# Two tiles' q in one pass group, and the projection moved to q's bank

## The chip, the cores and the metric

One core of a Trainium2 chip. The time is that of one execution on the device, in microseconds; lower is better. Five engines work side by side with queues of their own: TensorE (PE; its weight loads are shown as PEld), VectorE (DVE), ScalarE (ACT), GpSimd (POOL), and SyncE (SP), which starts the DMA transfers. They meet only by semaphores.

## The reference

The input is 8 images of 256 channels, 56 x 56, float32. Layer 0: `x = x + conv3x3(gn(x))`, where `gn` normalizes over 32 groups of 8 channels. Layer 1: `x = x + attention(gn(x))`. The attention works in windows of 4 x 4 pixels (16 tokens), 196 windows an image:

```python
qkv    = einsum('nchw,oc->nohw', windows, qkv_w)        # 256 -> 768 channels
pooled = avg_pool5(qkv)                                 # inside the window, sum / 25
q, k, v = relu(...), relu(...), ...                     # 64 groups of 8 channels: 32 of qkv, 32 of pooled
kv  = einsum('ngld,nglm->ngdm', k, [v, 1])
out = einsum('ngld,ngdm->nglm', q, kv);  out = out[..., :-1] / (out[..., -1:] + 1e-15)
y   = proj_w @ out                                      # 512 -> 256 channels, then batch norm
```

## The kernel before, in words

The images are done one after the other. An image has two parts. The **convolution** runs in 4 chunks of 14 rows, each as 4 products (a transform of the three columns of taps saves a third of the work); a product is, for each half `mt` of the output channels, 18 TensorE passes of 392 columns. Its operands are float32 values divided into a high and a low part (`F32R`, one pass each), and high x high, high x low and low x high are added (`PARTS`). The **attention** runs over 25 tiles (`TILES`) of 8 windows, 128 tokens; the last, tile 24, has 4 windows, 64 tokens. Products of the next image's first chunks are laid beside the ends of the attention: product halves stand in tiles 0, 22, 23 and 24, and `first_chunk` mixes the first tiles' work with the next image's first products. The last image has no products left; there `keep_warm` fills the beginning.

TensorE's order in a turn of the attention (`tile`, turn s): `attend` (q of tile s times its kv; 64 small matmuls of two passes), `keys_times_values` for tile s+1, `q_of_tile` for tile s+2, `turn` (transposes what VectorE divided, `ao`), `pooled` (pooling of tile s+2's keys and values), `project` of tile s-1, `keys_values` of tile s+3. Turns 1 to 20 are a hardware loop of 10 rounds with two turns each; the others are written out. `at_slot` places the code of some turns at an offset (`SLOT_...`). A float32 matmul, as in `q_of_tile` and `project`, is two passes in the trace; one with F32R operands is one.

ScalarE in turn s: `pooled_q` of s+1 (two instructions out of `qsum`), `turned` (the copy of the transposed result to `at`), `pooled_keys_values` of s+2, `q_of_tile` of s+2 (a raw copy to `qraw`, and two masked relus from PSUM), `batch_norm` of s-1, `split_tile` of s+4 (high part of the normalized tile), `keys_values` of s+3. VectorE: `weights` and `outputs` of s (den, rcp, ao), `kv_low_part` of s+2, two `mask` of s+1, `normalize_tile` and `tile_low` of s+4. A tile whose 8 windows cross a row of 14 windows is normalized and added in 4 instructions, another in 2; tiles 1, 3, 5, 8, 10, 12, 15, 17, 19 and 22 cross one. GpSimd: `spread_pooled` of s+2 (pooled v into `ve`), `pool_q` of s+2 (7 instructions that sum q over 5 x 5 inside a window), `add_tile` of s-1.

PSUM has 8 banks of 512 float32: q in bank 0, keys and values in 1, attention's output in 2 and 3, keys times values in 4 to 7, the project result in the free columns of 4 and 5 (`Y0`).

Of the kernel before, what the change touches and what calls it, by code (L numbers as in the profile page):

```python
# [86 lines left out]
Y0 = 2 * PLACES * QW  # L87


def conv_bank(v, mt):  # L90

    c, kk = v // len(PRODUCTS) % CONV_CHUNKS, v % len(PRODUCTS)
    if v < CONV_STEPS:
        return BANK_C[kk % 2][mt]
    if (c, kk) == (0, len(PRODUCTS) - 1):
        return (BANK_O, BANK_Q)[mt]
    if (c, kk) == (1, 0):
        return (BANK_KV, BANK_Q)[mt]
    if (c, kk) == (1, 2):
        return BANK_O + mt  # L100
    return BANK_C[kk % 2][mt]
# [26 lines left out]
STATS_AT = {(1 + (i + 1) // 4, (i + 1) % 4): i for i in range(CHUNKS)}  # L128
LOOPED = TILES - 5
# [3 lines left out]
SLOT_LEAD, SLOT_FIRST, SLOT_LOOP, SLOT_OUT = 152, 80, 92, (80, 56)  # L133
# [12 lines left out]
def build(nc, x, w_conv, w_q, w_kv, w_proj, bn, gavg, pool_m, ident, hmask, vinit, out):  # L146
    ctx = ExitStack()
    with ctx:
# [7 lines left out]
        wq = sb("wq", [P, KT, C])  # L156
# [30 lines left out]
        xt = sb("xt", [P, 2, 2, KT, TT], F32R)  # L187
        qraw = sb("qraw", [P, MT * TT])
        qh = sb("qh", [P, MT * TT])
        qm = sb("qm", [P, MT * TT // WS])  # L190
        qsum = sb("qsum", [P, MT * TT])
# [16 lines left out]
        poolm_raw = kvm_flat[0:TT, KT * 2 * C:KT * 2 * C + TT]  # L208
        wspace = xs[:, 1].rearrange("p k n -> p (k n)")
# [81 lines left out]
        def _(sp):  # L291
# [41 lines left out]
        def _(pe):  # L333
# [87 lines left out]
            def project(e, units):  # L421
                n = units * TT // 2
                for mt in range(MT):
                    for q in range(QUADS):
                        last = nc.tensor.matmul(ps[:, BANK_A + mt, Y0:Y0 + n],  # L425
                                                wp[:, q, mt * P:(mt + 1) * P], at[:, q, e, 0:n],
                                                start=(q == 0), stop=(q == QUADS - 1))
                last.then_inc(proj_done, 1)
# [9 lines left out]
            def tile(T, e, s=None, v=None):  # L438
# [10 lines left out]
                masks, own_mask = held(pe, T * 2 + 2), held(pe, T * 2 + 3)  # L449
# [19 lines left out]
                half = None if v is None else {0: (v - 1, 1), TILES - 3: (v, 0), TILES - 2: (v, 1),  # L469
                                               TILES - 1: (v + 1, 0)}.get(s)  # L470
# [38 lines left out]
            def attention(b):  # L509
                t0 = b * TILES  # L510
                v = (b + 1) * CONV_STEPS + len(PRODUCTS) if b + 1 < B else None
                pe.wait_ge(q_ready, t0 + 1)
                q_of_tile(1)
# [9 lines left out]
                for s in range(FIRST_LOOPED):  # L523
                    tile(t0 + s, s % 2, s, v)
                at_slot(SLOT_LOOP)
                with pe.Fori(0, LOOPED // 2) as i:
                    for e in range(2):
                        tile(t0 + i * 2 + (FIRST_LOOPED + e), (FIRST_LOOPED + e) % 2)
                for s in range(FIRST_LOOPED + LOOPED, TILES):
                    if s - FIRST_LOOPED - LOOPED < len(SLOT_OUT):  # L530
                        at_slot(SLOT_OUT[s - FIRST_LOOPED - LOOPED])
                    tile(t0 + s, s % 2, s, v)
# [6 lines left out]
            def first_tile(b):  # L539
                pe.wait_ge(xh_low, b * TILES + 1)  # L540
                keys_values(b * TILES + 1, 0)
                pe.wait_ge(y_ready, b * TILES + 1)
                q_of_tile(0)

            def second_tile(b):
                pe.wait_ge(xh_low, b * TILES + 2)
                pe.wait_ge(vp_raw, b * TILES + 1)
                keys_values(b * TILES + 2, 1)

            def later_chunks(b):  # L550


                for c in range(1, CONV_CHUNKS):
                    for kk in range(len(PRODUCTS)):
# [7 lines left out]
                        if b >= 1 and (c, kk) == (2, 0):  # L562
                            pe.wait_ge(y_ready, b * TILES + 1)
# [57 lines left out]
        def _(act):  # L621
# [16 lines left out]
            def split_tile(b, t):  # L638
# [3 lines left out]
                nc.scalar.copy(xt[:, 0, t % 2], xh[:, t % 2]).then_inc(xh_high, 1)  # L642
# [23 lines left out]

            def q_of_tile(b, t):

                act.wait_ge(q_done, b * TILES + t + 1)
                if t >= 1:  # L670
                    act.wait_ge(qsum_ready, b * TILES + t)
                nc.scalar.copy(qraw[:], ps[:, BANK_Q, 0:MT * TT]).then_inc(qraw_ready, 1)  # L672
                if t >= 2:
                    act.wait_ge(att_done, b * TILES + t - 1)
                for a in range(2):
                    last = nc.scalar.activation(
                        qs[:, 0:MT, t % 2, :].rearrange("p m (w a t) -> p m w a t", a=2, t=TOK)[:, :, :, a, :],
                        ps[:, BANK_Q, 0:MT * TT].rearrange("p (m w t) -> p m w t", m=MT, t=TOK),
# [597 lines left out]
```

## Time and profile before

| | |
|---|---|
| time, median of 3 | 2419.68 us (2418.15 to 2420.84) |
| the profiled execution | 2419.14 us, span 2417.3 us |
| PE busy | 2366.7 us, 98% |
| DVE busy | 1730.8 us, 72% |
| ACT busy | 1451.0 us, 60% |
| POOL busy | 1170.9 us, 48% |

The busy time of PE is modelled and counts passes that overlap once; what is busy all the time need not be at its peak. The chain of waits goes back from the last instruction to whatever released each step. The shares are means over convolution and attention: ScalarE and GpSimd have nearly all their work in the attention.

### The profile page before, as it was taken

How to read it: one execution, taken by the hardware profiler on the slowest of the kernel's cores; microseconds unless marked ns; L12 is line 12 of the kernel's file. 1: busy time of each engine (PE TensorE's matmuls, PEld its weight loads, DVE VectorE, ACT ScalarE, POOL GpSimd, SP SyncE). 2: the span in 40 equal slices, each digit the busy share in tenths (PEclk: the TensorE clock that was granted, in tenths of full speed). 3: DMA queues.
4: the chain of work that ended last, by engine and by line, in shares of the span. 5: the costliest groups of instructions: out<-in, count | busy, mean ns of one | idle time of the engine just before them, and what ended most of it. 6: DMA issues, size and time to landing. Idle time of an engine off the chain costs nothing.

```text
span 2417.3 us, 112385 instructions
## 1 busy us (share of the span) xinstructions
PE 2366.7 (98%) x49576; PEld 2150.9 (89%) x49576; DVE 1730.8 (72%) x3206; ACT 1451.0 (60%) x3754; POOL 1170.9 (48%) x2365
## 2 busy tenths in 40 slices
PE   7999999999999999999999999999999999998998
PEld 7998899888998889988899888998889988897887
DVE  9887658767587765877658766687766876665764
ACT  2158861588516884178832788327882288813886
POOL 0037750477405773057730677216771167712776
PEclk9999999999999999999999999999999999999999
DMA  4000010000200001000010000100001000000000
GB/s 171 1 2 16 19 65 10 2 19 16 75 1 6 15 20 71 1 6 19 16 71 1 7 18 16 71 1 9 16 20 66 1 9 19 21 9 2 16 16 25
DMA packets 39114, 58.37 MB, mean 24 GB/s; under 512 B 4704, under 2 KB 36064, under 8 KB 36832
## 3 DMA queue, kind: packets, MB, share of 16 engines
q1 hardware_dynamic: 38880, 55.27, 6.4%
q8 instruction: 144, 2.36, 0.4%
q14 instruction: 90, 0.74, 0.1%
HBM read 29.57 MB, written 25.69 MB: 23 GB/s over the span
## 4 chain that ended last, share of the span: by engine, by line
PE 95%; DVE 2%; issue 1%; DMA 0%; ACT 0%; SPq 0%; POOL 0%; POOLq 0%; DVEq 0%
PE ps L354 33%; PE ps L425 15%; PE ps L373 12%; PE ps L414 10%; PE ps L400 9%; PE ps L380 9%; PE ps L389 4%; PE ps L434 3%; DVE dp L883 1%; DMA xs<-w_conv 0%; PE ps L336 0%; DVE xs L896 0%; DVE kv_part L989 0%; PE ps L365 0%; DVE rcp L999 0%
## 5 line engine op out<-in xcount | busy, mean ns | idle before, releaser
L354 PE MATMUL ps<-dp,wc 128*128 128x392 f32 x4608 | 840.8, 341 | 0.2 <-DVE dp L883 0.2
L354 PEld LDWEIGHTS ps<-dp,wc 128*128 128x128 f32 x4608 | 815.3, 188 | 5.3 <-issue 3.1
L1204 POOL TENSOR_TENSOR ve<-vpraw,vmask 128x1024 f32<-128x1024 f32 x200 | 381.0, 1905 | 349.8 <-ACT vpraw L665 349.8
L425 PEld LDWEIGHTS ps<-at,wp 128*128 128x128 f32 x3200 | 373.1, 191 | 47.5 <-DVE kvm L1016 46.4
L425 PE MATMUL ps<-at,wp 128*128 128x128 f32 (+1 forms) x3200 | 404.7, 280 | 1.0 <-ACT yb L700 1.0
L1175 POOL TENSOR_TENSOR qm<-qraw 128x64 f32<-128x64 f32 x200 | 59.5, 298 | 700.5 <-ACT qraw L672 699.9
L636 ACT CAST dp<-dt 128x896 fp32r<-128x896 f32 x128 | 121.0, 945 | 449.0 <-PE ps L354 356.3
L373 PE MATMUL ps<-wkv,xt 128*128 128x512 f32 x1200 | 324.8, 406 | 1.6 <-issue 1.6
L654 ACT ACTIVATE ve<-ps,vmask 128x256 f32<-128x256 f32 x800 | 314.3, 491 | 0.0
L414 PEld LDWEIGHTS ps<-kvm,qs 64*32 64x32 f32 x25088 | 233.5, 105 | 90.8 <-issue 88.8
L1016 DVE TENSOR_TENSOR kvm<-ps,hm 128x576 f32<-128x576 f32 (+1 forms) x400 | 277.4, 734 | 2.9 <-PE ps L400 2.8
L976 DVE TENSOR_SCALAR xh<-xs,gn 128x128 f32<-128x128 f32 (+3 forms) x560 | 278.1, 550 | 1.6 <-PE ps L380 1.3
L984 DVE TENSOR_TENSOR xt<-xh,xt 128x256 fp32r<-128x256 f32 x200 | 108.6, 543 | 236.2 <-ACT xt L642 236.1
L414 PE MATMUL ps<-kvm,qs 64*32 64x36 f32 x25088 | 261.0, 204 | 17.0 <-issue 16.5
L896 DVE TENSOR_TENSOR xs<-xs,ps 128x392 f32<-128x392 f32 x384 | 199.8, 556 | 92.4 <-PE ps L354 91.7
L1215 POOL TENSOR_TENSOR xs<-yb,xs 128x128 f32<-128x128 f32 (+3 forms) x560 | 202.7, 389 | 114.6 <-ACT yb L700 114.6
L400 PE MATMUL ps<-ve,kr 64*32 64x144 f32 x12544 | 246.3, 285 | 1.0 <-issue 1.0
L373 PEld LDWEIGHTS ps<-wkv,xt 128*128 128x128 f32 x1200 | 211.7, 189 | 37.6 <-issue 2.6
L688 ACT ACTIVATE qs<-qsum,qmaskp 128x256 f32<-128x256 f32 x400 | 182.2, 504 | 89.6 <-POOL qsum L1194 89.6
L380 PEld LDWEIGHTS ps<-xh,wq 128*128 128x128 f32 x1600 | 194.3, 191 | 43.4 <-issue 41.4
L997 DVE TENSOR_SCALAR den<-ps 128x64 f32<-128x64 f32 (+1 forms) x200 | 44.5, 223 | 260.0 <-PE ps L414 260.0
L380 PE MATMUL ps<-xh,wq 128*128 128x128 f32 x1600 | 230.1, 287 | 0.0
(86 smaller groups left out, 3110.3 us busy)
## 6 DMA issues: line engine op xcount, KB each, us to landing
out<-xs SPq DMA_DIRECT2D x224, 112.0 KB, 1.8
xs<-x SPq DMA_DIRECT2D x14, 1344.0 KB, 7.5
xs<-x SPq DMA_DIRECT2D x14, 224.0 KB, 2.7
xs<-w_conv SPq DMA_DIRECT2D x2, 1152.0 KB, 12.2
xs<-x SPq DMA_DIRECT2D x2, 896.0 KB, 6.6
xs<-x SPq DMA_DIRECT2D x2, 672.0 KB, 7.8
kvm<-w_kv SPq DMA_DIRECT2D x1, 512.0 KB, 13.7
wp<-w_proj SPq DMA_DIRECT2D x4, 128.0 KB, 9.9
```

Source lines behind the costliest of these rows:

```text
L354: last = nc.tensor.matmul(ps[:, conv_bank(v, mt), 0:CONV_N], wc[:, part_w, k, kt * TAPS + dy, mt * P:(mt + 1) * P], dp[:, kk % 2, part_d, ...
L373: last = nc.tensor.matmul(ps[0:TT, BANK_KV, :], xt[:, part_x, e, kt, :], wkv[:, part_w, kt, :], start=(i == 0 and kt == 0), stop=(i == len ...
L380: last = nc.tensor.matmul(ps[:, BANK_Q, mt * TT:(mt + 1) * TT], wq[:, kt, mt * P:(mt + 1) * P], xh[:, e, kt, :], start=(kt == 0), stop=(kt ...
L400: last = nc.tensor.matmul(ps[32 * q:32 * q + 32, BANK_A + 2 * h + r, gg * PLACES * QW:(gg + 1) * PLACES * QW], kr[64 * r:64 * r + 64, e, k ...
L414: last = nc.tensor.matmul(ps[32 * c:32 * c + 32, BANK_O + r, (u * G + g) * QW:(u * G + g + 1) * QW], qs[64 * r:64 * r + 64, g, e, w * 32:w ...
L425: last = nc.tensor.matmul(ps[:, BANK_A + mt, Y0:Y0 + n], wp[:, q, mt * P:(mt + 1) * P], at[:, q, e, 0:n], start=(q == 0), stop=(q == QUADS ...
L654: last = nc.scalar.activation(ve[:, t % 2, e, 0].rearrange("p (n m) -> p n m", m=DIM + 1)[:, :, 0:DIM], ps[0:TT, BANK_KV, C:2 * C].rearran ...
L896: last = nc.vector.tensor_tensor(pair[:, :, e], pair[:, :, e], ps[:, conv_bank(v, mt), 0:CONV_N], op)
L976: last = nc.vector.tensor_scalar(xh[:, t % 2, kt, first * TOK:(first + n) * TOK].rearrange("p (w r c) -> p w r c", r=WS, c=WS), xs_row(b, ...
L1016: nc.vector.tensor_tensor(kvm[:, h, 0:n].rearrange("p r (g c) -> p r g c", g=2), ps[:, BANK_A + 2 * h:BANK_A + 2 * h + n, 0:2 * PLACES * Q ...
L1204: nc.gpsimd.tensor_tensor(ve[:, t % 2, :, 1].rearrange("p e (n m) -> p e n m", m=DIM + 1)[:, :, :, 0:DIM], vpraw[:].rearrange("p (n m) -> ...
L1215: last = nc.gpsimd.tensor_tensor(xrow, yb[:, t % 2, mt, first * TOK:(first + n) * TOK].rearrange("p (w r c) -> p w r c", r=WS, c=WS), xrow ...
```

## The change

q is computed for a pair of tiles (2i, 2i+1) at once, from the high and low parts that keys and values already use, with q's weights divided into two parts too: 12 passes a pair of 256 columns (64 in the last, half-filled pair). TensorE does it in even turns (in turn 0 behind `pooled`). `project` writes to q's bank; in even turns it stands where it stood, in odd turns its first half of output channels stands in q's old place and the second half where project stood. ScalarE copies q raw once a pair, and both q relus read that copy; GpSimd sums q once a pair over twice the data, behind `spread_pooled`. In odd turns ScalarE does `q_of_tile` first and `pooled_q` only after `pooled_keys_values`. In tile 24 the product comes after `turn`. The last product of a chunk 0 and the first ones of chunk 1 use other banks. `at_slot` offsets change.

```diff
-Y0 = 2 * PLACES * QW
     if (c, kk) == (1, 0):
-        return (BANK_KV, BANK_Q)[mt]
-    if (c, kk) == (1, 2):
-        return BANK_O + mt
+        return (BANK_KV, BANK_C[0][1])[mt]
+PAIRS_Q = -(-TILES // 2)
-SLOT_LEAD, SLOT_FIRST, SLOT_LOOP, SLOT_OUT = 152, 80, 92, (80, 56)
+SLOT_LEAD, SLOT_FIRST, SLOT_LOOP, SLOT_OUT = 160, 80, 92, (88, 40)
-        wq = sb("wq", [P, KT, C])
+        wq = sb("wq", [P, 2, KT, C], F32R)
...
@@ TensorE
-            def q_of_tile(e):
-                for mt in range(MT):
-                    for kt in range(KT):
-                        last = nc.tensor.matmul(ps[:, BANK_Q, mt * TT:(mt + 1) * TT],
-                                                wq[:, kt, mt * P:(mt + 1) * P], xh[:, e, kt, :],
-                                                start=(kt == 0), stop=(kt == KT - 1))
+            def q_of_pair(tokens=2 * TT):
+                for mt in range(MT):
+                    for i, (part_w, part_x) in enumerate(PARTS):
+                        for kt in range(KT):
+                            last = nc.tensor.matmul(
+                                ps[:, BANK_Q, mt * 2 * TT:mt * 2 * TT + tokens],
+                                wq[:, part_w, kt, mt * P:(mt + 1) * P],
+                                xt[:, part_x, kt, :, :].rearrange("p e t -> p (e t)")[:, 0:tokens],
+                                start=(i == 0 and kt == 0), stop=(i == len(PARTS) - 1 and kt == KT - 1))
                 last.then_inc(q_done, 1)
...
-            def project(e, units):
+            def project(e, units, mts=range(MT)):
...
-                        last = nc.tensor.matmul(ps[:, BANK_A + mt, Y0:Y0 + n],
+                        last = nc.tensor.matmul(ps[:, BANK_Q, mt * TT:mt * TT + n],
...
@@ tile, after attend and keys_times_values
-                    if is_tile(-2):
-                        pe.wait_ge(y_ready, n0)
...
                 if half and s == 0:
-                    pe.wait_ge(q_ready, n2)
+                    pe.wait_ge(qraw_ready, pairs - 1)
                     product(*half)
-                elif is_tile(2):
-                    pe.wait_ge(q_ready, n2)
-                    q_of_tile(e)
-                elif half:
-                    pe.wait_ge(q_ready, n2 if is_tile(1) else n1)
+                if e == 0:
+                    if is_tile(2) and s != 0:
+                        if is_tile(3):
+                            pe.wait_ge(xh_low, n4)
+                        pe.wait_ge(y_ready, n0)
+                        q_of_pair(2 * TT if is_tile(3) else TT // 2)
+                elif is_tile(-1):
+                    pe.wait_ge(qraw_ready, pairs)
+                    if is_tile(-2):
+                        pe.wait_ge(y_ready, n0)
+                    project(1 - e, 2, (0,) if is_tile(2) else range(MT))
+                if half and s == TILES - 2:
+                    pe.wait_ge(masked, masks)
                     product(*half)
                 pe.wait_ge(ao_ready, n1)
                 turn(units(0))
                 if is_tile(2):
                     pooled(n3)
-                if half and s == 0:
-                    pe.wait_ge(conv_added, 2 * v + 4)
-                    q_of_tile(e)
-                if is_tile(-1):
-                    if is_tile(1):
-                        pe.wait_ge(masked, own_mask)
+                if e == 1 and is_tile(-1) and is_tile(2):
+                    project(1 - e, 2, (1,))
+                if s == 0:
+                    if half:
+                        pe.wait_ge(conv_added, 2 * v + 4)
+                    pe.wait_ge(xh_low, n4)
+                    pe.wait_ge(qraw_ready, pairs - 1)
+                    q_of_pair()
+                if half and s == TILES - 1:
+                    product(*half)
+                if e == 0 and is_tile(-1):
+                    if is_tile(2):
+                        pe.wait_ge(qraw_ready, pairs)
                     else:
                         pe.wait_ge(y_ready, n0)
                     project(1 - e, 2)
...
@@ first_tile: q_of_tile(0) goes; second_tile: q_of_pair() between its wait and keys_values; attention: q_of_tile(1) goes
...
@@ ScalarE, attention(b)
-                    if s + 1 < TILES:
+                    if s % 2 == 0 and s + 1 < TILES:
                         pooled_q(b, s + 1)
...
+                    if s % 2:
+                        if 0 <= s and s + 2 < TILES:
+                            q_of_tile(b, s + 2)
+                        if s >= 0:
+                            turned(b, s)
+                        if 0 <= s < TILES - 2:
+                            pooled_keys_values(b, s + 2)
+                        pooled_q(b, s + 1)
+                        if s >= 1:
+                            batch_norm(b, s - 1)
+                    else:
+                        if 0 < s and s + 2 < TILES:
+                            q_of_pair(b, s // 2 + 1)
+                        if s >= 0:
+                            turned(b, s)
+                        if 0 <= s < TILES - 2:
+                            pooled_keys_values(b, s + 2)
+                        if s == 0:
+                            q_of_pair(b, 1)
+                        if s + 2 < TILES:
+                            q_of_tile(b, s + 2)
+                        if s >= 1:
+                            batch_norm(b, s - 1)
...
@@ GpSimd
+                spread_pooled(b, 0)
                 pool_q(b, 0)
-                spread_pooled(b, 0)
                 spread_pooled(b, 1)
-                for s in range(-1, TILES):
-                    if 0 <= s < TILES - 2:
+                for s in range(TILES):
+                    if s < TILES - 2:
                         spread_pooled(b, s + 2)
-                    if s + 2 < TILES:
-                        pool_q(b, s + 2)
+                    if s % 2 == 0 and s + 2 < TILES:
+                        pool_q(b, s // 2 + 1)
                     if 1 <= s:
                         add_tile(b, s - 1)
```

## Rows read from the trace of the kernel before

**Rows 1.** The page, chain that ended last: shares of the span by engine.
```profile
PE 95%; DVE 2%; issue 1%; DMA 0%; ACT 0%; SPq 0%; POOL 0%; POOLq 0%; DVEq 0%
```
**Rows 2.** Windows, first image's loop: us, busy of PE, PEld, DVE, ACT, POOL, PEclk.
```profile
192.30:320.90 128.60, 128.60 (x3879) 111.20 (x3879) 90.19 (x167) 112.25 (x307) 98.20 (x202) 1.00 0.05 17
```
**Rows 3.** The chain in order of time, one loop turn: start us, us, what.
```profile
804.88 1.88 PE ps L425 x16
806.76 1.39 PE ps L373 x6
808.15 1.23 PE ps L414 x80
809.38 1.07 PE ps L400 x64
810.45 1.09 PE ps L380 x8
811.54 0.44 PE ps L434 x4
811.98 0.46 PE ps L389 x2
```
**Rows 4.** The chain: runs of passes of convolution, q and project.
```profile
359.82 44.88 PE ps L354 x252
438.96 0.89 PE ps L380 x8
642.59 1.79 PE ps L425 x16
```
**Rows 5.** Groups by shape, project of half tiles: busy us, mean ns, idle before.
```profile
L425 PE MATMUL ps<-at,wp 128*128 128x64 f32 x128 | 15.2, 272 | 1.0 <-ACT yb L700 1.0
```
**Rows 6.** Timeline, one loop turn: start us, us, engine line op, [idle before <-releaser].
```profile
805.24 2.62 DVE L976 TENSOR_SCALAR xh<-xs,gn 128x64 f32<-128x64 f32 x4
807.51 0.29 POOL L1175 TENSOR_TENSOR qm<-qraw 128x64 f32<-128x64 f32 x1
807.88 0.41 ACT L642 CAST xt<-xh 128x256 fp32r<-128x256 f32 x1 [0.28 <-DVE xh L976]
808.20 0.58 ACT L649 CAST kv_part<-ps 128x512 fp32r<-128x512 f32 x1
808.95 1.57 ACT L654 ACTIVATE ve<-ps,vmask 128x256 f32<-128x256 f32 x4
809.42 0.23 DVE L997 TENSOR_SCALAR den<-ps 128x64 f32<-128x64 f32 x1 [0.59 <-PE ps L414]
810.26 0.69 DVE L1007 TENSOR_TENSOR ao<-ps,rcp 128x512 f32<-128x512 f32 x1
810.35 0.43 POOL L1194 TENSOR_TENSOR qsum<-qsum,qh 128x128 f32<-128x128 f32 x1
810.81 0.91 ACT L688 ACTIVATE qs<-qsum,qmaskp 128x256 f32<-128x256 f32 x2 [0.29 <-POOL qsum L1194]
811.80 0.65 ACT L708 COPY at<-ps 128x256 f32<-128x256 f32 x2
```
**Rows 7.** Groups by shape, GpSimd, 200 to 320 us: busy us, mean ns.
```profile
L1204 POOL TENSOR_TENSOR ve<-vpraw,vmask 128x1024 f32<-128x1024 f32 x16 | 30.6, 1910 | 22.3 <-ACT vpraw L665 22.3
L1194 POOL TENSOR_TENSOR qsum<-qsum,qh 128x128 f32<-128x128 f32 x16 | 6.8, 425 | 1.3
L1191 POOL TENSOR_TENSOR qsum<-qm,qh 128x64 f32<-128x64 f32 x16 | 5.1, 320 | 1.3
```
**Rows 8.** Timeline, last image, tile 24: the transposes.
```profile
2408.09 0.44 PE L434 MATMUL ps<-idn,ao 128*128 128x128 f32 x2 [1.13 <-DVE ao L1007]
```
**Rows 9.** Timeline, second image: the masks before tile 0, pooling in tile 2.
```profile
453.65 1.40 DVE L1016 TENSOR_TENSOR kvm<-ps,hm 128x576 f32<-128x576 f32 x2
478.18 0.74 PE L389 MATMUL ps<-kv_part,poolm 128*128 128x512 f32 x2 [0.66 <-DVE kv_part L989]
```
**Rows 10.** The chain, second image, tile 1, first turn of the loop.
```profile
465.46 1.02 issue
```

More of the change, by code:

```diff
@@ L186, in build @@
         xh = sb("xh", [P, 2, KT, TT])
[L187 to L191, printed above, removed]
+        xt = sb("xt", [P, 2, KT, 2, TT], F32R)
+        qraw = sb("qraw", [P, MT * 2 * TT])
+        qh = sb("qh", [P, MT * 2 * TT])
+        qm = sb("qm", [P, MT * 2 * TT // WS])
+        qsum = sb("qsum", [P, MT * 2 * TT])
         qs = sb("qs", [P, G, 2, 2 * TT])
@@ L419, in attend @@
                 last.then_inc(att_done, 1)
-            def project(e, units):
+            def project(e, units, mts=range(MT)):
                 n = units * TT // 2
-                for mt in range(MT):
+                for mt in mts:
                     for q in range(QUADS):
-                        last = nc.tensor.matmul(ps[:, BANK_A + mt, Y0:Y0 + n],
+                        last = nc.tensor.matmul(ps[:, BANK_Q, mt * TT:mt * TT + n],
                                                 wp[:, q, mt * P:(mt + 1) * P], at[:, q, e, 0:n],
                                                 start=(q == 0), stop=(q == QUADS - 1))
-                last.then_inc(proj_done, 1)
+                if mt == MT - 1:
+                    last.then_inc(proj_done, 1)
             def turn(units):
@@ L436, in turn, with tile @@
                     last.then_inc(tr_done, 1)
-            def tile(T, e, s=None, v=None):
+            def tile(T, pair, e, s=None, v=None):
                 def is_tile(d):
@@ L448, in tile @@
                 n0, n1, n2, n3, n4 = [held(pe, T + d) for d in range(5)]
-                masks, own_mask = held(pe, T * 2 + 2), held(pe, T * 2 + 3)
+                masks, pairs = held(pe, T * 2 + 2), held(pe, pair + 1)
+                half = None if v is None else {0: (v - 1, 1), TILES - 3: (v, 0), TILES - 2: (v, 1),
+                                               TILES - 1: (v + 1, 0)}.get(s)
                 pe.wait_ge(w_loaded, DMA)
@@ L523, in attention @@
                 for s in range(FIRST_LOOPED):
-                    tile(t0 + s, s % 2, s, v)
+                    tile(t0 + s, p0 + s // 2, s % 2, s, v)
                 at_slot(SLOT_LOOP)
@@ L527, in attention @@
                     for e in range(2):
-                        tile(t0 + i * 2 + (FIRST_LOOPED + e), (FIRST_LOOPED + e) % 2)
+                        tile(t0 + i * 2 + (FIRST_LOOPED + e), p0 + i + (FIRST_LOOPED + e) // 2, (FIRST_LOOPED + e) % 2)
                 for s in range(FIRST_LOOPED + LOOPED, TILES):
@@ L531, in attention @@
                         at_slot(SLOT_OUT[s - FIRST_LOOPED - LOOPED])
-                    tile(t0 + s, s % 2, s, v)
+                    tile(t0 + s, p0 + s // 2, s % 2, s, v)
             def last_tile(b):
@@ L641, in split_tile @@
                     act.wait_ge(kv_done, b * TILES + t - 1)
-                nc.scalar.copy(xt[:, 0, t % 2], xh[:, t % 2]).then_inc(xh_high, 1)
+                    act.wait_ge(q_done, b * PAIRS_Q + t // 2)
+                nc.scalar.copy(xt[:, 0, :, t % 2, :], xh[:, t % 2]).then_inc(xh_high, 1)
             def keys_values(b, t):
@@ L699, in batch_norm @@
                 for mt in range(MT):
[L700 removed]
+                    last = nc.scalar.activation(yb[:, t % 2, mt, 0:n], ps[:, BANK_Q, mt * TT:mt * TT + n],
                                                 ACT.Identity, bias=bns[:, mt:mt + 1], scale=bni[:, mt:mt + 1])
@@ L750, in first_chunk @@
                 keys_values(b, 0)
-                q_of_tile(b, 0)
                 pooled_keys_values(b, 0)
                 split(v + 4)
+                q_of_pair(b, 0)
                 split_tile(b, 2)
                 keys_values(b, 1)
+                for t in range(2):
+                    q_of_tile(b, t)
                 pooled_keys_values(b, 1)
@@ L776, in _ @@
             act.wait_ge(c_loaded, CONSTS * DMA)
-            nc.scalar.copy(wkv[:, 0], wkv_raw).then_inc(att_w_high, 1)
+            nc.scalar.copy(wkv[:, 0], wkv_raw)
+            nc.scalar.copy(wq[:, 0], wq_raw).then_inc(att_w_high, 1)
             nc.scalar.copy(poolm[:], poolm_raw).then_inc(y_ready, 1)
@@ L791, in _ @@
                     keys_values(b, 0)
-                    q_of_tile(b, 0)
                     pooled_keys_values(b, 0)
+                    q_of_pair(b, 0)
                     split_tile(b, 2)
                     keys_values(b, 1)
+                    for t in range(2):
+                        q_of_tile(b, t)
                     pooled_keys_values(b, 1)
```

75 lines of the change are left out of this document (35 added, 40 removed).

## The prediction

> **What bounds the kernel now.** I read the chain of waits first, then the busy shares of a stretch inside the attention loop, then that stretch in order of time. The reader should see in [rows 1] that the chain is TensorE for 95% of the span, and in [rows 2] that in 128.6 us of the loop (17 tiles) TensorE is busy for all of it, ScalarE for 112.25 us, GpSimd for 98.20 and VectorE for 90.19. Per tile that is 7.56, 6.60, 5.78 and 5.31 us. So only what takes time off TensorE pays, but ScalarE has less than 1 us per tile to give away. [rows 3] is one tile on TensorE: project 1.88, keys and values 1.39, attend 1.23, keys times values 1.07, q 1.09, turn 0.44, pooling 0.46; they follow each other without a gap and repeat every 7.56 us (811.98 + 0.46 - 804.88). The granted clock of that stretch is 1.00, the 2.4 GHz level [rows 2].
>
> **The passes of q, the gain.** Before, a tile's q is 8 float32 passes of 128 columns, so 16 a pair. Where nothing small runs before it, 8 take 0.89, 0.111 each; 16 passes of the same shape in project take 1.79, 0.112 each [rows 4]. After, a pair is 2 x 3 x 2 = 12 single passes of 256 columns. No such pass is in the trace. The single passes that are there: 392 columns, 44.88/252 = 0.178 us [rows 4]; 512 columns, 1.39/6 = 0.232 [rows 3]. The line through both gives 0.178 - 136 x 0.00045 = 0.117. From below it could be 0.107 (one column a cycle at 2.4 GHz, by which 392 columns are 0.163 of their 0.178), from above 0.178, the nearest longer pass. I take 0.116, by the line. A pair: 16 x 0.112 - 12 x 0.116 = 1.79 - 1.39 = 0.40 less.
>
> The last pair has one half tile, 64 columns. Float32 passes of 64 columns take 15.2/128 = 0.119 each [rows 5], no less than those of 128, so something other than columns, the load of 128 x 128 weights by all likelihood, sets about 0.112. Then 12 passes cost 12 x 0.112 = 1.34 against 8 x 0.111 = 0.89: 0.45 more. Per image 12 x 0.40 - 0.45 = 4.35 less, times 8: **-34.8 us**. Bounds: at 0.107 a pass 96 x 12 x 0.009 = 10 us more gain; at 0.178, 96 x 12 x 0.062 = 71 us of loss.
>
> After keys-times-values q takes 1.09 and not 0.89 [rows 3, 4]: 0.20 goes when the small tiles end and full passes begin. That crossing stays once in every turn, before q in even turns, before the first half of project in odd ones; I count nothing, with a gain of 88 x 0.20 = 18 us as its other end (11 odd turns x 8), if project, whose operands are older, crosses for nothing.
>
> Rule against this change: the Trainium skill, TensorE: Matmul & The Clock Gate, Part 3, The mechanism, says that a weight load overlaps running matmuls only when its row group differs, and its section on LDWEIGHTS gives P/1.2, 107 ns for 128 columns. By it a 256-column pass would be 107 + 107 = 0.214 us and the change would lose 96 x 12 x 0.098 = 113 us against my sum. The trace disagrees: a full 128 x 128 pass of 392 columns repeats every 0.178 us [rows 4], where that rule makes 0.27.
>
> **The order of a pair.** Even turn on TensorE: attend 1.23, keys-times-values 1.07, q pair 1.39 + 0.20, turn 0.44, pooled 0.47, project 1.88, keys 1.39: 8.07. Odd: 1.23 + 1.07 + half project 0.20 + 0.94 + turn 0.44 + pooled 0.47 + half project 0.94 (0.20 is in the before's q; project's split itself is free) + keys 1.39: 6.68. Sum 14.75 against 15.13. I laid the other engines beside it, 0 being the start of the even attend, with durations and lags from [rows 6]:
> - VectorE: weights start 1.27 after attend starts (809.42 against 808.15), ao is done at 2.80 (810.95). The turn comes at 3.89 in the even turn and at 8.07 + 3.44 in the odd one, against 3.39 before: no wait. Normalizing a tile that crosses a row has 2.62 us; in an odd turn it ends some 0.6 after the turn does (it starts 4.65 into a turn, as before). ScalarE's split and keys then come 1 us late, at 1.0 of the even turn. Values are ready at 3.3, their low part at 4.1, the pooling at 4.33: covered by 0.2. The low tile is ready at 1.7, q pair wants it at 2.30: covered by 0.6. Such tiles are 3 in 7 and never adjacent, so the lag does not add up.
> - ScalarE, even: keys until 2.3 (start 0.05, 0.75 + 1.5), pooled q 3.2, waits for q pair at 3.9, raw copy (512 wide, 0.58 as the copy of the same size in [rows 6]) 4.5, turned 5.1, pooled keys 5.7, q from the copy 6.5, batch norm 7.5, split 7.9, keys at 8.1. The project at 4.8 needs the raw copy at 4.5. Odd: keys until 10.4, q 11.2, turned from 11.8 to 12.4, pooled keys 13.0, pooled q 13.9, batch norm 14.6, split 14.9, keys. It gives one raw copy less per pair (0.38 twice against 0.58). The even attend at 14.75 needs pooled q of 13.9: covered by 0.8, which is also all that the late place of pooled q leaves.
> - GpSimd: the spread waits for pooled v at 5.7 and takes 1.9 [rows 7], to 7.7, and only then the sums of q begin. They span 3.27 now (807.51 to 810.78). Doubled data: 64 to 128 elements cost 0.10 more [rows 7], so six instructions +0.10 and the two wide ones +0.2 each, 4.3 in all; bounds 3.3 and 6.54 (twice). They end at 12.0, ScalarE asks at 13.0. The next spread: 13.1 to 15.2, wanted at 16.6.
> So the loop runs at TensorE's pace. Moving project to q's bank adds waits on the raw copy, on batch norm (two turns old) and drops that on the mask; by the times above each is met early. The split of wq's weights (one copy on ScalarE, one subtraction on VectorE) falls under the first image's convolution, where TensorE has no gap; cost nothing, 0.6 each without cover. SP's queue is unchanged. Convolution banks: the product that sat in bank 0 moves to bank 5, free at that time: nothing.
>
> **The end of attention, a loss.** Tile 23 is odd, and ScalarE now does turned(23) and after it the pooled q of tile 24; TensorE does nothing between turn(23) and attend(24), since project(22) has moved ahead. turned takes 0.65, pooled q of a half tile some 0.6, against 0.22 of head start by the first half of the turn and 0.1 of latency: 1.1 us of wait, in 7 images. In the last image no product lengthens tile 23, and the q sums (ready 5.8 + 1.9 + 4.3 = 12.0, then 0.7) meet an attend at 6.7 + 1.23 + 0.55 + 2.08 + 0.44 = 11.0: 1.8 us. In tile 24 turn comes right behind attend, where before a product (18 passes, 3.2 us) lay between: the last image, which never had that product, shows what that costs, 1.13 us [rows 8]; now in the other 7 too. Together 7 x 1.1 + 1.8 + 7 x 1.13 = **+17.4 us**. Behind the waiting attend and turn stand the product and project of TensorE, so nothing takes it back. Bounds 0 to 25.
>
> **The beginning.** q(1) no longer stands between the first keys-times-values and the first attend; the masks (1.40, from 0.5 behind it, [rows 9]) end 1.9 after it, keys fill 1.4: +0.45 x 7 = +3.2. In the last image turn(0) has no q ahead of it: +0.7. In tile 2 the pooling waited 0.66 us [rows 9]; q pair is 0.5 longer than q and covers that much: -0.5 x 7 = -3.5. Sum **+0.4**.
>
> Total -34.8 + 17.4 + 0.4 = -17.0. The profiled execution took 2419.14 us (span 2417.3), 0.5 under the median of 2419.68: 2402 us.
>
> **Rivals.**
> 1. The tail or the crossing is cheaper than I say (0.20 saved in odd turns, the ends covered): 2402 - 18 = 2384. For it: project's inputs are long ready. Against: the crossing shows wherever small tiles precede. 0.13.
> 2. The odd turn is too short for VectorE and ScalarE: 4 odd turns of an image (tiles 5, 15, 17, 19 normalized) come 1 us late, my covers there are 0.2; if each loses 0.6, 4 x 8 x 0.6 = 19: 2421, no change. 0.12.
> 3. Slower: GpSimd's sums decide. From 6.1 us on (14.75 - 0.9 - 7.7) each microsecond is paid once a pair; at 6.54, with the semaphore lags, attend waits 0.5 in 88 pairs: 2402 + 44 = 2446. For it: the spread stands ahead of the sums, and ScalarE waits 0.29 us for sums today already [rows 6]. Against: the small growth in [rows 7]. 0.12.
> 4. Slower: code loading. A gap of 1.02 us stands where the loop is entered [rows 10], none in the iterations after. With new positions one could recur in all 80 iterations: 2402 + 80 = 2482. 0.05. Passes of 0.178 instead of 0.116 would give 2473: 0.02.
> 5. Slower: the load of the weights is not hidden behind a single pass: 0.112 + 0.107 = 0.219 a pass, 96 x 12 x 0.103 = 119 us: 2521. Against it stands the 0.178 of 392 columns [rows 4]. 0.01.
>
> The Trainium skill's rule on weight loads, cited above, is this case.
>
> My forecast has 0.55. About 0.2% (4.8 us) is what can be told from no change. Faster 0.55 + 0.13 and a little of case 2, less the upper edge of my own: 0.69; same 0.10; slower 0.21. Range 2380 to 2432: case 1 and its passes of 0.107 below, case 2 and half of case 3 above.
>
> **What would show it.** Two turns of the loop at 14.7 us; q's 12 passes in 1.4 (+0.2); project in odd turns 1.1 and 0.95; GpSimd's sums 4.3 us a pair; waits of TensorE only around tiles 0 and 24, about 1.1 us ahead of attend(24) and ahead of turn(24). Wrong: a wait of attend on ScalarE's pooled q in each pair, or a pass above 0.13 us.

## The result, and the profile after

The changed kernel takes 2440.12 us (median of 4, 2435.93 to 2441.23) against 2419.86 (2418.15 to 2420.84): a ratio of 1.0084, 95% interval 1.0069 to 1.0100. It is slower, by 0.84%. The profiled execution took 2435.93 us, 16.8 more than that of before.

The page of the changed kernel: instructions, TensorE's busy time, and the chain by engine.
```profile
span 2434.0 us, 110819 instructions
PE 2347.7 (96%) x49224; PEld 2139.7 (88%) x49224; DVE 1694.7 (70%) x3207; ACT 1421.5 (58%) x3659; POOL 1039.4 (43%) x1597
PE 90%; DVE 5%; issue 2%; ACT 1%; DMA 0%; SPq 0%; POOL 0%; POOLq 0%; ACTq 0%; DVEq 0%
```
TensorE has 19 us less to do and stands idle 86.3 us (2434.0 - 2347.7), 35.7 more than before. In [rows 1] the chain was TensorE for 95%; now VectorE, ScalarE and "issue" have 8% together. Before any gap is looked at, the loop. The chain of the changed kernel, an even turn's end and two turns (start, us, what):
```profile
199.61 1.81 PE ps L428 x16
201.42 1.39 PE ps L372 x6
202.81 1.23 PE ps L417 x80
204.04 1.07 PE ps L403 x64
205.11 1.09 PE ps L428 x8
206.20 0.44 PE ps L438 x4
206.64 0.47 PE ps L392 x2
207.10 0.89 PE ps L428 x8
207.99 1.53 PE ps L372 x6
209.52 1.23 PE ps L417 x77
210.75 1.07 PE ps L403 x64
211.82 1.62 PE ps L381 x12
213.44 0.44 PE ps L438 x4
213.88 0.47 PE ps L392 x2
214.35 1.82 PE ps L428 x16
```
Two turns take 14.74 us (214.35 - 199.61), against 15.13 from [rows 3]. The 12 passes of q take 1.62 behind the small tiles, half a project 1.09 behind them and 0.89 elsewhere. So far all is as forecast. What went wrong is elsewhere, and the starts of five groups in the chain of the second image show where:
```profile
362.45 44.88 PE ps L353 x252
...
440.21 0.93 PE ps L372 x4
...
484.57 0.47 PE ps L372 x2
...
618.40 1.40 PE ps L372 x6
...
659.92 44.88 PE ps L353 x252
```
| stretch of the second image | before | after |
|---|---|---|
| convolution, to the keys of tile 0 | 77.76 | 77.76 |
| from there to the keys issued in turn 2 | 43.32 | 44.36 |
| turn 2 to turn 20, nine pairs | 136.13 | 133.83 |
| turn 20 to the next convolution | 38.38 | 41.52 |
| sum | 295.59 | 297.47 |

The same five in the kernel before are at 359.82 [rows 4], 437.58, 480.90, 617.03 and 655.41. The loop gains 2.3 us, its beginning loses 1.0 and the end 3.1. The timeline of the changed kernel has all idle stretches of TensorE above 0.15 us in that image (in brackets: idle time and its releaser):
```profile
458.84 1.29 PE L417 MATMUL ps<-kvm,qs 64*32 64x36 f32 x128 [0.71 <-issue]
473.86 1.63 PE L372 MATMUL ps<-wkv,xt 128*128 128x512 f32 x6 [0.27 <-issue]
478.46 0.30 PE L417 MATMUL ps<-kvm,qs 64*32 64x36 f32 x16 [1.88 <-issue]
586.28 0.73 PE L392 MATMUL ps<-kv_part,poolm 128*128 128x512 f32 x2 [0.24 <-DVE kv_part L1034]
621.57 0.60 PE L417 MATMUL ps<-kvm,qs 64*32 64x36 f32 x45 [0.94 <-issue]
629.46 0.33 PE L417 MATMUL ps<-kvm,qs 64*32 64x36 f32 x21 [0.71 <-issue]
647.64 0.76 PE L417 MATMUL ps<-kvm,qs 64*32 64x36 f32 x64 [1.31 <-ACT qs L713]
649.52 0.44 PE L438 MATMUL ps<-idn,ao 128*128 128x128 f32 x2 [1.13 <-DVE ao L1052]
```
The last two are attend(24) and turn(24), as forecast. The first is attend(0). The second, 0.27, is a wait as well, though it is marked "issue": the keys wait for ScalarE's `vpraw`, and the gap ends 0.10 us after that has ended (473.33 + 0.43), as it does in the same place of the six other images:
```profile
473.33 0.43 ACT L681 ACTIVATE vpraw<-ps 128x256 f32<-128x256 f32 x1
```
The three others marked "issue", in the loop's first round (turn 2) and behind the loop (tiles 21 and 22), are 3.53 us (1.88 + 0.94 + 0.71), where the kernel before had 1.02 [rows 10], 0.22 and 0.40; no term of the prediction holds them. Over the whole run TensorE's idle time marked "issue" is 38.3 us against 19.1; of that, the gaps that stand inside a run of small passes are 31.5 against 17.5.

### The profile page after: what moved, and what is told of

Its sections match the earlier page's. It is cut to its first block, busy times and chain, and to the rows that moved or that the text cites. A ratio compares the mean times of both kernels' runs of the same rounds, so it can differ in the third digit from the quotient of the medians.

```text
span 2434.0 us, 110819 instructions
## 1 busy us (share of the span) xinstructions
PE 2347.7 (96%) x49224; PEld 2139.7 (88%) x49224; DVE 1694.7 (70%) x3207; ACT 1421.5 (58%) x3659; POOL 1039.4 (43%) x1597
## 4 chain that ended last, share of the span: by engine, by line
PE 90%; DVE 5%; issue 2%; ACT 1%; DMA 0%; SPq 0%; POOL 0%; POOLq 0%; ACTq 0%; DVEq 0%
PE ps L353 33%; PE ps L428 15%; PE ps L372 11%; PE ps L417 10%; PE ps L403 8%; PE ps L381 6%; PE ps L392 4%; PE ps L438 3%; DVE xh L1021 1%; DVE kv_part L1034 1%; ACT ve L670 1%; DVE ao L1052 1%; DVE dp L929 0%; DVE rcp L1044 0%; DMA xs<-w_conv 0%
## 5 line engine op out<-in xcount | busy, mean ns | idle before, releaser
L1250 POOL TENSOR_TENSOR ve<-vpraw,vmask 128x1024 f32<-128x1024 f32 x200 | 385.9, 1930 | 1207.1 <-ACT vpraw L681 1207.1
L428 PEld LDWEIGHTS ps<-at,wp 128*128 128x128 f32 x3200 | 387.4, 191 | 49.0 <-issue 24.7
L428 PE MATMUL ps<-at,wp 128*128 128x128 f32 (+1 forms) x3200 | 417.2, 279 | 1.1 <-ACT yb L726 1.0
L1021 DVE TENSOR_SCALAR xh<-xs,gn 128x128 f32<-128x128 f32 (+3 forms) x560 | 247.2, 496 | 0.3
L734 ACT COPY at<-ps 128x256 f32<-128x256 f32 (+1 forms) x400 | 129.6, 381 | 152.5 <-PE ps L438 152.5
L726 ACT ACTIVATE yb<-ps,bns,bni 128x128 f32<-128x128 f32 (+1 forms) x400 | 160.9, 456 | 86.9 <-PE ps L428 86.9
L403 PEld LDWEIGHTS ps<-ve,kr 64*32 64x32 f32 x12544 | 192.2, 105 | 4.2 <-issue 4.2
L699 ACT ACTIVATE qs<-qraw,qmask 128x256 f32<-128x256 f32 (+1 forms) x400 | 184.7, 535 | 0.9 <-PE ps L417 0.6
```

Source lines behind the costliest of these rows:

```text
L403: last = nc.tensor.matmul(ps[32 * q:32 * q + 32, BANK_A + 2 * h + r, gg * PLACES * QW:(gg + 1) * PLACES * QW], kr[64 * r:64 * r + 64, e, k ...
L428: last = nc.tensor.matmul(ps[:, BANK_Q, mt * TT:mt * TT + n], wp[:, q, mt * P:(mt + 1) * P], at[:, q, e, 0:n], start=(q == 0), stop=(q == ...
L699: last = nc.scalar.activation(qs[:, 0:MT, t % 2, 0:2 * n].rearrange("p m (w a t) -> p m w a t", a=2, t=TOK)[:, :, :, a, :], qraw[:].rearra ...
L1021: last = nc.vector.tensor_scalar(xh[:, t % 2, kt, first * TOK:(first + n) * TOK].rearrange("p (w r c) -> p w r c", r=WS, c=WS), xs_row(b, ...
L1250: nc.gpsimd.tensor_tensor(ve[:, t % 2, :, 1].rearrange("p e (n m) -> p e n m", m=DIM + 1)[:, :, :, 0:DIM], vpraw[:].rearrange("p (n m) -> ...
```

## The experiments

Theory A: the pair pays; what is lost lies in waits at the ends of attention, in gaps that depend on where the code lies, and in drops of TensorE's clock behind such gaps. Rival B: the pair's schedule itself costs. For the gaps, A1: they follow the code's place; A2: they come from waits. Of a run with one timing I give that time beside the kernel before in the same session.

**e1, the tail in order again.** In `tile` and in ScalarE's turn 23:
```diff
-                    project(1 - e, 2, (0,) if is_tile(2) else range(MT))
+                    project(1 - e, 2, (0,))          # tile 23: first half alone
-                if half and s == TILES - 2:
+                if half and s >= TILES - 2:          # product of tile 24 ahead of turn
...
-                if e == 1 and is_tile(-1) and is_tile(2):
+                if e == 1 and is_tile(-1):           # tile 23: second half behind turn
                     project(1 - e, 2, (1,))
...
-                if half and s == TILES - 1:
-                    product(*half)
...
+                        if s == TILES - 2:
+                            pooled_q(b, s + 1)       # ahead of turned
```


> The changed kernel with the end of attention put back in order: in tile 24 the product lies before the transposes again, in tile 23 half of project follows the transposes, and ScalarE does the pooled q of tile 24 before turned(23). Theory A (the q pair pays, the loss is in waits at the ends, in gaps of instruction supply, and in clock drops that these bring): the waits of 1.31 and 1.13 us an image go, 7 x 2.44 + 1.3 = 18 us, and the clock drops behind them, some 2 to 4 us: 2418 to 2422 against 2440. Theory B (the pair's own schedule is what is slower, and the ends only show it): the time moves by less than 8 us, and new waits appear in the loop.

Measured: 2417.21 (2413.09 to 2422.45) beside 2417.66, ratio 1.0001 (0.9991 to 1.0010); from 1.0084 that is 20 us. The timeline of e1 at tiles 23 and 24:
```profile
640.59 0.60 PE L438 MATMUL ps<-idn,ao 128*128 128x128 f32 x4
641.02 1.06 PE L428 MATMUL ps<-at,wp 128*128 128x128 f32 x8
642.01 0.77 PE L417 MATMUL ps<-kvm,qs 64*32 64x36 f32 x64
642.76 3.44 PE L353 MATMUL ps<-dp,wc 128*128 128x392 f32 x18
646.03 0.38 PE L438 MATMUL ps<-idn,ao 128*128 128x128 f32 x2
```
No bracket is left; no new wait came in the loop. A is right in size (18), B is not. The clock drops did not go with the waits: the mean granted clock of the profiled execution is 0.995 here and 0.996 in the changed kernel, so the 20 us are the waits alone (TensorE's idle time fell by 19.5 us).

**e4, the same from the other side:** the kernel before, with only tile 24's product behind the transposes.
```diff
-                elif half:
+                elif half and s < TILES - 1:
                     pe.wait_ge(q_ready, n2 if is_tile(1) else n1)
                     product(*half)
                 pe.wait_ge(ao_ready, n1)
                 turn(units(0))
+                if half and s == TILES - 1:
+                    product(*half)
```


> The kernel before with one part of the change alone: in tile 24 the product comes after the transposes. Theory A: VectorE's ao is then waited for, 1.1 us in 7 images, +8 us, 2427 to 2429, and up to 4 us more if the clock drops behind it. Theory B: the product only changes place, 2420 within 3 us.

Measured: 2426.17 (2423.96 to 2427.19) beside 2417.66, ratio 1.0033 (1.0021 to 1.0046), 8.5 us. The timeline of e4, tile 24:
```profile
646.57 0.44 PE L434 MATMUL ps<-idn,ao 128*128 128x128 f32 x2 [1.13 <-DVE ao L1009]
```
The wait of [rows 8] stood in the last image, where no product lay between; here it is in all eight, the same 1.13.

**e2 and e3, offsets exchanged.** The one line each:
```diff
-SLOT_LEAD, SLOT_FIRST, SLOT_LOOP, SLOT_OUT = 160, 80, 92, (88, 40)     # changed kernel, e2
+SLOT_LEAD, SLOT_FIRST, SLOT_LOOP, SLOT_OUT = 152, 80, 92, (80, 56)     # e3 has the reverse, in the kernel before
```


> The changed kernel with the code offsets of the kernel before (152, 80, 92, (80, 56)). Theory A1 (the gaps marked issue, 4.5 us an image against 1.7 before, follow from where the code lies): the gaps ahead of attend(0), in tiles 21 and 22 change in size by 0.3 us and more each, the one in tile 2 (offset unchanged) stays 1.6 to 1.9; the time moves by 3 to 15 us either way. Theory A2 (the gaps come from waits or register work, not from the place of the code): every gap stays within 0.1 us and the time within 3 us of 2440.

> The kernel before with the code offsets of the changed one (160, 80, 92, (88, 40)). A1: gaps of tiles 21 and 22 (0.22 and 0.40 before) and possibly one ahead of attend(0) change; if the new offsets fit only the new code, 2419.7 + 2 to 10 us. A2: 2419.7 within 3 us, gaps unchanged.

Measured: e2 2441.17, ratio 1.010 (1.008 to 1.012), against 1.0084 of the changed kernel: not told apart, where A1 expected 3 us or more. e3 2420.24, ratio 1.0011 (1.0000 to 1.0022). In the second image e2 has 0.91 us in tile 21 (0.94 in the changed kernel), 1.34 in tile 22 with 29 passes left (0.71 with 21) and 0.68 ahead of attend(0) (0.71); e3 has 0.61 in tile 21 (0.22 in the kernel before) and none in tile 22 (0.40). But one image is not enough to read a size from. The place of a gap is the same in all eight images of a run, its size is not: 0.59 to 1.07 us in tile 21 of the changed kernel, 0.20 to 0.78 in the kernel before. Means of the eight images:

| | tile 21 | tile 22 |
|---|---|---|
| changed kernel (88, 40) | 0.81 | 0.92 |
| e2 (80, 56) | 0.61 | 1.03 |
| kernel before (80, 56) | 0.49 | four of 8 images above 0.15 |
| e3 (88, 40) | 0.53 | one of 8 images above 0.15 |

The passes left move with the offset, so A2 falls as far as the place goes. That the size moved by 0.3 us, as A1 had it, is not shown. And the sum marked "issue" stays with the kernel and not with the offsets: 37.9 us in e2 (38.3 at the new offsets), 20.6 in e3 (19.1 at the old ones). So the choice of offsets is not why the changed kernel has nearly twice the gaps; what else of its code is, no run shows.

**e5 to e8, offsets alone, on e1.** LEAD, FIRST, LOOP, OUT of e1: 160, 80, 92, (88, 40).
```diff
+SLOT_LEAD, SLOT_FIRST, SLOT_LOOP, SLOT_OUT = 100, 80, 60, (120, 80)     # e5
+SLOT_LEAD, SLOT_FIRST, SLOT_LOOP, SLOT_OUT = 200, 80, 130, (40, 0)      # e6
+SLOT_LEAD, SLOT_FIRST, SLOT_LOOP, SLOT_OUT = 240, 80, 0, (0, 120)       # e7
+SLOT_LEAD, SLOT_FIRST, SLOT_LOOP, SLOT_OUT = 40, 80, 180, (160, 160)    # e8
```


> The kernel of e1 with code offsets 100, 80, 60, (120, 80). A gap stands where attend's passes cross a multiple of 256 instructions: at offset 88 with 45 of 128 passes left, at 80 with 41, at 40 with 21, at 56 with 29, so a pass is two instructions. Theory A1: at 120 tile 21's gap stands with 61 passes left, tile 22's (80) with 41 left, and each gap grows as less of attend lies ahead of the crossing; total of gaps other than 36.8 us by 5 us or more. Theory A2 (the place does not matter): gaps of e1, 0.70, 0.31, 1.60, 0.76, 0.98 us an image.

> The kernel of e1 with code offsets 200, 80, 130, (40, 0). A1: tile 21's gap with 21 passes left, tile 22's at the very end or none; the loop's gap in tile 2 moves in the passes and changes by 0.3 us or more. A2: as e1.

> The kernel of e1 with code offsets 240, 80, 0, (0, 120). A1: no crossing inside tile 21's attend, the gap falls between attend and keys-times-values and is small or none; tile 22's with 61 passes left; the loop's first gap changes. A2: as e1.

> The kernel of e1 with code offsets 40, 80, 180, (160, 160). A1: crossings early in attend (81 passes left), gaps the largest of the four kernels, 45 us in all or more, time 2425 or more. A2: as e1, 2417 within 4 us.

Measured, beside 2415.48: e5 2438.36, e6 2469.18, e7 2451.04, e8 2523.30. The instructions and waits are e1's; only their addresses differ. The loop's middle is the same in all (attend to attend 6.7 us in an odd turn, 8.05 in an even one and 8.28, 8.17 and 8.59 in turns 12, 14 and 16, to 0.03); entry and exit differ. e5, tile 21 at offset 120, then tile 22 at 80:
```profile
629.53 0.73 PE L417 MATMUL ps<-kvm,qs 64*32 64x36 f32 x61 [0.86 <-issue]
639.25 0.57 PE L417 MATMUL ps<-kvm,qs 64*32 64x36 f32 x41 [1.08 <-issue]
```
e7, tile 22 at 120, and e6, tile 22 at 0:
```profile
631.77 0.81 PE L417 MATMUL ps<-kvm,qs 64*32 64x36 f32 x61 [1.74 <-issue]
```
```profile
638.49 0.22 PE L417 MATMUL ps<-kvm,qs 64*32 64x36 f32 x1 [1.26 <-issue]
```
The passes left are 61 at 120, 45 at 88, 41 at 80, 29 at 56, 21 at 40, 1 at 0: the position is that of the next multiple of 256 instructions at two a pass, (256 - 88 - 2)/2 = 83 of 128 done at 88. At offset 160 (e8) it gives 81 left, and at the offsets of the later runs, 20, 28, 60 and 70, it gives 11, 15, 31 and 36 left; the traces have just these. The Trainium skill, Runtime: NRT & Kernel Launch, section Instruction fetch mechanics, has instructions arrive in blocks of 256, the next fetched while the current one runs. The places of the gaps agree with such blocks; no run shows the fetch itself. At these offsets gaps stand in other runs of passes too: in keys times values in e6 to e8, in project in e5, in q in e7 and e8. The size of a gap does not follow from the offset alone: 0.86 and 1.74 both at 120, and over all images 0.53 to 1.11 in tile 21 of e5, 1.20 to 1.76 in tile 22 of e7. One expectation failed: at offset 40 in e6 tile 21 has no gap at all in this image, and at most 0.22 in the others. The sum of TensorE's idle time marked "issue" was 36.8 us in e1 and 54.4, 65.3, 59.2 and 90.2 here. In e8 it is half (53) of the 106 us that e8 is slower than e1; the other half is about what the clock took, 0.975 in the mean against 0.995 (an estimate: 0.020 x 2520 = 50 us). Each of the four ran once; the smallest difference to e1 is 21 us, and the ten executions of e1 lie within 10 us.

**The clock.** The windows of the changed kernel around turn 2 of the third image (us, then PE, PEld, DVE, ACT, POOL busy, PEclk, DMA share, GB/s):
```profile
774.00:776.00 2.00, 0.10 (x13) 0.07 (x14) 0.00 (x0) 2.00 (x6) 0.21 (x1) 1.00 0.02 4
777.00:778.00 1.00, 1.00 (x28) 0.78 (x10) 0.96 (x3) 0.00 (x0) 0.00 (x0) 0.70 0.06 16
778.00:779.00 1.00, 1.00 (x6) 1.00 (x6) 1.00 (x2) 0.00 (x0) 0.00 (x0) 0.50 0.00 0
779.00:780.00 1.00, 1.00 (x7) 1.00 (x6) 1.00 (x2) 0.00 (x0) 0.00 (x0) 0.50 0.00 0
781.00:782.00 1.00, 1.00 (x9) 0.94 (x8) 0.31 (x2) 0.91 (x4) 0.00 (x0) 1.00 0.00 0
```
Behind a gap of 1.9 us in turn 2 the granted clock stands at 0.5 (1.2 GHz) from 777.4 to 780.8: half of 3.4 us is lost. In the changed kernel that happens at 777.4 and 2258.8 behind turn 2, at 948.1 and 1842.4 behind the two waits of tile 24, and at 2217.8 where the last image's statistics are waited for; the kernel before has the last of these alone, at 2203.7 (each has one more in its last 2 us). Four more drops, some 7 us. Not each gap brings one: only 1 of the 7 gaps of turn 2 ahead of the last image did here.

**e9 to e12, the masks earlier.** In `first_chunk`, VectorE, on e1 (`add_product` gets an argument that names its parts); then offsets again:
```diff
-                add_product(v + 3, 0)
+                add_product(v + 3, 0, (0,))      # the sums alone
                 mask(b, 0, 0)
                 mask(b, 0, 1)
+                add_product(v + 3, 0, (1,))      # their statistics
...
+SLOT_LEAD, SLOT_FIRST, SLOT_LOOP, SLOT_OUT = 160, 80, 92, (40, 40)     # e9
+SLOT_LEAD, SLOT_FIRST, SLOT_LOOP, SLOT_OUT = 150, 80, 40, (40, 20)     # e10
+SLOT_LEAD, SLOT_FIRST, SLOT_LOOP, SLOT_OUT = 130, 80, 76, (40, 56)     # e11
+SLOT_LEAD, SLOT_FIRST, SLOT_LOOP, SLOT_OUT = 170, 80, 20, (20, 60)     # e12
```


> e1 with the first masks ahead of the convolution's statistics on VectorE in first_chunk, offsets 160, 80, 92, (40, 40). If the 0.70 us ahead of attend(0), the same at all six offsets, is the masks and not the code, it falls to 0.1 to 0.2. By tile 21 of e6 (offset 40: its turn 6.72 us against 7.59 at 88) that turn is 6.7 to 6.9. Time 2406 to 2414.

> e9 with offsets 150, 80, 40, (40, 20). The crossing in the loop's entry moves; tiles 1 and 2 together, 17.34 us in e1 and 17.63 at offset 0, take 17.0 to 18.0. Another number than e9's is all that the place of the code would mean.

> e9 with offsets 130, 80, 76, (40, 56). Offset 60 gave tiles 1 and 2 19.19 us, 92 gave 17.34: between them, 17.3 to 18.5.

> e9 with offsets 170, 80, 20, (20, 60). Tiles 1 and 2 17.3 to 17.8 (near offset 0), tile 21 6.7 to 7.0, tile 0 above 10.0 as LEAD passes 160.

Measured, beside 2417.6: e9 2413.70, e10 2436.62, e11 2422.72, e12 2411.28. e1 and e9, the first attend:
```profile
454.55 1.29 PE L417 MATMUL ps<-kvm,qs 64*32 64x36 f32 x128 [0.70 <-issue]
```
```profile
453.78 1.64 PE L372 MATMUL ps<-wkv,xt 128*128 128x512 f32 x6
455.36 1.40 PE L417 MATMUL ps<-kvm,qs 64*32 64x36 f32 x128
```
So this 0.7 us was the wait for the masks, though the profile calls it "issue". Turns 1 and 2 together took 18.8 us in e9, 17.8 in e10 (as expected), 19.0 in e11 (expected up to 18.5) and 19.6 in e12 (up to 17.8: missed); e9, e11 and e12 had a clock drop in that very turn. Turn 21 took 7.10 in e9 (6.9 at most expected) and 7.08 in e12 (7.0 at most), and tile 0 9.8 in e12 (above 10.0 expected): three small misses. That e12 is the fastest of the four is in part luck: its execution had three drops ahead of its last 2 us, mean clock 0.998, and the same code had 0.994 to 0.999 in the nine executions of e13.

**e13 to e15, the best version timed.** e13 is e12's code; e14 and e15:
```diff
+SLOT_LEAD, SLOT_FIRST, SLOT_LOOP, SLOT_OUT = 130, 80, 92, (20, 60)     # e14
+SLOT_LEAD, SLOT_FIRST, SLOT_LOOP, SLOT_OUT = 170, 80, 8, (28, 70)      # e15
```


> The kernel of e12 again, timed. Theory A (q pair pays 0.36 us a pair, the rest was ends and code): 2409 to 2413 against 2417 to 2420 of before, a ratio of 0.996 to 0.998 with an interval below 1. Rival (the first look was lucky with the clock, the pair is worth nothing): ratio 0.999 to 1.001.

> e13 with LEAD 130 and LOOP 92, the exit as it is. If the loop's entry matters little between 20 and 92 (tiles 1 and 2 without a clock drop: 17.3 at 92, 17.6 at 0), 2408 to 2414 and the gaps in tiles 21 to 23 as in e12, 0.2, 1.1, 1.0.

> e13 with LOOP 8 and exit offsets 28 and 70. Tile 21 stays near 0.2; a crossing of tile 22's attend with 35 passes left, gap 0.9 to 1.2 as at 60; 2406 to 2416.

Measured: e13 2411.38 (2406.39 to 2416.84) beside 2415.69, ratio 0.9981 (0.9971 to 0.9991); e14 2414.94, 0.9994 (0.9985 to 1.0004), the same as before and just above its 2408 to 2414; e15 2414.76, once, its tile 22 gap 1.95 in the second image where 0.9 to 1.2 was expected (0.85 to 1.40 in the others). With its ends repaired and the masks moved the kernel with the pair of q is faster than the kernel before, by 0.19%, some 4.5 us, a little less than the 0.2% to 0.4% that was expected. It is not repaired whole: it still has 35.0 us marked "issue" against 19.1, so the offsets found took none of the gaps away.

The nine executions of e13 also show what the clock takes, since their code is one and the same: the three fastest, 2406.39, 2408.78 and 2408.78 us, had a mean granted clock of 0.999 and 0.998, the two slowest, 2416.71 and 2416.84, had 0.994. The kernel before had 0.998 to 1.000 in all 19 executions beside them, with 2415.69 as their median. At an equal clock of 0.999 the new kernel is thus some 7 to 9 us faster (an estimate from two executions), and about half of that goes to its drops.

One comparison is missing: twelve sets of offsets were run with the pair, and the kernel before got only its own and one other. Whether it would gain from others too is not shown.

## Why the prediction was wrong

- **The passes**: right. 0.116 a pass was forecast; 12 take 1.44 to 1.46, 0.121, where nothing small precedes (the chain, 440 to 470 us), 1.62 behind small tiles (1.59 forecast). Two turns: 14.74 against 14.75. The sum used 0.40 a pair, though the prediction's own order of a pair gives 15.13 - 14.75 = 0.38. The crossing of 0.20 was not saved (half a project 1.09 behind small tiles, 0.89 elsewhere), so rival 1 did not come. The 12 passes of 64 columns take 1.46, 1.34 forecast, no less than those of 256. The rule on weight loads of the Trainium skill (TensorE: Matmul & The Clock Gate, Part 3, The mechanism), by which a pass would be 0.214, does not hold here: it is 0.121. So rival 5 did not come either.
- **The other engines in the loop**: right for GpSimd, wrong for the crossing tiles. GpSimd's sums of a pair, the rival with the highest price, in the timeline of the changed kernel:
```profile
202.37 0.41 POOL L1221 TENSOR_TENSOR qm<-qraw 128x128 f32<-128x128 f32 x1
206.42 0.67 POOL L1240 TENSOR_TENSOR qsum<-qsum,qh 128x256 f32<-128x256 f32 x1
207.68 0.91 ACT L713 ACTIVATE qs<-qsum,qmaskp 128x256 f32<-128x256 f32 x2
```
  4.72 us (202.37 to 207.09) against 4.3 forecast, done 0.6 before ScalarE begins: rival 3 did not come. Rival 2 did, in small. The even turns 12, 14 and 16 of the second image, each behind an odd turn in which a crossing tile (15, 17, 19) was normalized, take 8.29, 8.18 and 8.59 us from attend to attend, the other even turns 8.05 to 8.10: 0.9 us an image, where the sum had "covered by 0.2". The brackets show little of it (0.24 at 586.28), but the chain of turn 16 runs back as the rival has it, from pooling to the values' low part, to ScalarE's values and to VectorE's normalizing (a few small pieces are left out):
```profile
579.68 3.15 DVE xh L1021 x4
...
584.04 1.47 ACT ve L670 x4
...
585.53 0.70 DVE kv_part L1034
...
586.28 0.73 PE ps L392 x2
```
  The other turns make 14.77 a pair; nine pairs would be 132.9 and took 133.8.
- **The end of attention**: right, 1.31 and 1.13 an image against 1.1 and 1.13. e1 gives it back, e4 brings the wait of turn(24), about half of it, to the kernel before. In the last image 1.31, not 1.8.
- **The beginning**: the wait for the masks is 0.71, not 0.45, and the wait for `vpraw` in turn 1 (0.27 in the second image, 1.7 in all) was not seen.
- **The step that failed** is the sum's silence on the gaps that go with the code's place: they were put at nothing without a reason. Rival 4 put code loading as a gap in all 80 iterations or nothing. It came as a third thing: nearly the same few places as before, the loop's first round and the turns behind it, with gaps of 3.53 instead of 1.64 us in the second image. Over the run the gaps inside small passes are 31.5 against 17.5: 14 us, the largest single term that was missing. They had rows in the trace of before [rows 10], and the change takes passes out of the written-out turns and shifts them. Why they nearly doubled stays open (e2 and e3: not by the offsets). A term for them, 1.6 us an image now and 0 to 4 after, say, belonged into the sum; these bounds are chosen with hindsight, and would add up to 2.4 x 8 = 19 us.
- **The range** is not what it is said to be made of: case 2 and half of case 3 above 2402 are 2402 + 19 + 22 = 2443, and case 1 with passes of 0.107 is 2384 - 10 = 2374; 2380 to 2432 was stated. The measured 2440 lies inside the wider one, but that would have been luck: of the two cases only case 2 came, with some 7 us.
- **The clock**: not thought of. Some of those gaps and tail waits had a clock halved for 3.4 us behind them: some 7 us in the profiled execution.

From -17.0 to +16.8 there are 33.8 us: 14 of code gaps, 7 of clock, 7 of the loop's small waits (0.9 x 8), 2 of masks, 1 at the end of attention, 4 because a pair outside the crossing tiles gives 15.13 - 14.77 = 0.36 and not the 0.40 used (96 x 0.04), 1 for the last pair, less 1 in turn 2, where the wait of [rows 9] went whole (0.66, not 0.5). That is 35; it can be laid out no more exactly. Rival 4 had the right name; its form and its chance of 0.05 were wrong.

What stays open: why the changed code has nearly twice the gaps at either set of offsets, what sets a gap's size once its place is known (0.86 and 1.74 us at the same offset, and up to 0.8 us apart from image to image in one run), and which gaps bring a clock drop.

## What to carry to other kernels

In this kernel most gaps marked "issue" stand in runs of very short TensorE passes (128 in 1.23 us) of the written-out code and of a loop's first round, and moving the code by its offsets alone cost up to 106 us (e8 against e1, gaps and clock together). So a change that shifts written-out code beside a loop reprices its gaps: count those in the trace of before as a term with bounds of its own, and try several offsets before judging the change. First look whether such a gap ends just behind another engine's instruction: then it is a wait, and can be laid out as one. Where an order is rearranged for the steady state, lay the first and last turns beside it separately: here two moved steps at the end cost more than half of what the loop gained. And an idle gap of 1 to 2 us on TensorE can have a second price, in the clock behind it: here 1.7 us, in some images and not in others. A stretch covered by 0.2 us on paper is not covered.

## What the runs showed of the hardware that was not expected

- The same instructions took 2417 to 2523 us depending on the address of the code (e1 and e5 to e8), and with the masks earlier 2411 to 2437 (e9 to e15). Some 10 us of such a spread can be one code's own (e13: 2406 to 2417).
- In the small passes of tiles 21 and 22 a gap, where there is one, stands at a multiple of 256 instructions, with 61, 45, 41, 29, 21 and 1 of 128 passes left at offsets 120, 88, 80, 56, 40 and 0. In the same place its size differs from image to image (0.59 to 1.07 us in tile 21 of the changed kernel).
- The granted clock halved for 3.4 us behind a gap of 1.9 us or behind two waits of 1.31 and 1.13 us in a row, in some images and not in others.
- "issue" in the profile can be a wait: 0.70 us ahead of attend(0) went when VectorE's masks came earlier, and the gap ahead of the keys in turn 1 ends 0.10 us behind ScalarE's `vpraw` in seven images of seven.
